# Two layers on eight cores: attention preparation and attention interleaved one to one, and three score banks re-dealt

## The reference

```python
# q, k, v: 16 heads, D = 64, S = 2048; BQ = BKV = 64, scale = D ** -0.5
def step(carry, kv):
    o, m, l = carry
    s = einsum('bhnqd,bhkd->bhnqk', qb, kj) * scale
    m_new = maximum(m, s.max(axis=-1))
    p = exp(s - m_new[..., None])
    alpha = exp(m - m_new)
    l_new = alpha * l + p.sum(axis=-1)
    o_new = (alpha[..., None] * o + einsum('bhnqk,bhkd->bhnqd', p, vj)) / l_new[..., None]
...
return out @ Wo
```

## Time and profile before

| | us |
|---|---|
| runs, median of 2 | 10,394.06 |
| lowest and highest run | 10,362.76 and 10,425.37 |
| profiled execution | 10,050.02 |
| its span on the slowest core (core 3) | 10,048.5 |
| spans of the eight cores | 10,022.2 to 10,048.5 |
| busy in the span: TensorE, VectorE, ScalarE | 7585.1, 4055.9, 2167.9 |

### The profile page before, as it was taken

How to read it: one execution, slowest core, us unless ns; L and a number is a source line. 1 busy time by engine, 2 the same in 40 slices (tenths; PEclk the granted TensorE clock), 3 DMA queues, 4 the chain that set the end, 5 groups by cost and what they waited for, 6 DMA issues and landing times. The chain is left out here.

```text
span 10048.5 us, 90480 instructions; the slowest of 8 cores (10022.2 to 10048.5 us)
## 1 busy us (share of the span) xinstructions
PE 7585.1 (75%) x30432; PEld 2823.7 (28%) x30432; DVE 4055.9 (40%) x7403; ACT 2167.9 (22%) x3617; POOL 209.7 (2%) x256
## 2 busy tenths in 40 slices
PE   1688888888426464563746547999999999999998
PEld 0233333333101111110111102444444444444443
DVE  6433333432564545546455452233332323232332
ACT  0100001001024243342423334111111212111111
POOL 0000000000000000000000000000000000000000
PEclk6699999999655555565565556999999999999999
DMA  1121221211000000000000000222222222222222
GB/s 37 16 31 26 31 33 26 34 30 27 10 0 4 3 4 4 2 4 1 4 5 2 3 0 13 38 34 37 36 36 36 35 37 35 37 36 34 38 34 63
DMA packets 224606, 229.20 MB, mean 23 GB/s; under 512 B 23200, under 2 KB 220960, under 8 KB 222112
## 3 DMA queue, kind: packets, MB, share of 16 engines
q0 software_dynamic: 221280, 206.49, 13.7%
q1 hardware_dynamic: 2880, 16.94, 0.5%
HBM read 421.49 MB, written 8.39 MB: 43 GB/s over the span
## 5 line engine op out<-in xcount | busy, mean ns | idle before, releaser
L1387 PE MATMUL f_yb<-hh,ring 128*128 128x512 bf16 x8192 | 1820.0, 379 | 63.8 <-DVEq L99 52.1
L1354 PE MATMUL f_h<-xn,ring 128*128 128x512 bf16 x8192 | 1794.9, 381 | 30.7 <-issue 21.9
L1362 ACT ACTIVATE hh<-f_h,b_sb 128x512 bf16<-128x512 f32 x1024 | 703.6, 687 | 3036.1 <-PE f_h L1354 3036.1
L1035 PE MATMUL atb<-k,q 64*128 64x512 bf16 x1024 | 563.5, 591 | 878.2 <-ACT es L1052 872.3
L1399 DVE TENSOR_TENSOR x_sb<-x_sb,f_yb 128x512 f32<-128x512 f32 x1024 | 703.7, 687 | 1224.4 <-PE f_yb L1387 838.3
L1354 PEld LDWEIGHTS f_h<-xn,ring 128*128 128x128 bf16 x8192 | 800.8, 98 | 1022.3 <-issue 80.5
L1387 PEld LDWEIGHTS f_yb<-hh,ring 128*128 128x128 bf16 x8192 | 777.3, 98 | 1041.4 <-issue 146.3
L1057 DVE TENSOR_REDUCE sg<-es 128x8 f32<-128x512 f32 x1024 | 702.3, 686 | 815.6 <-ACT es L1052 815.6
L1368 DVE TENSOR_TENSOR hh<-hh,gb_sb 128x512 bf16<-128x512 bf16 x1024 | 435.3, 425 | 1410.1 <-ACT hh L1362 1410.1
L1052 ACT ACTIVATE es<-atb 128x512 f32<-128x512 f32 x1024 | 611.5, 597 | 1765.5 <-DVE mu L1042 1765.5
L1042 DVE TENSOR_REDUCE mu<-atb 128x8 f32<-128x512 f32 x1024 | 698.8, 682 | 596.0 <-PE atb L1035 596.0
(11 more groups left out here) (187 smaller groups left out, 4558.2 us busy)
## 6 DMA issues: line engine op xcount, KB each, us to landing
ring<-l1w POOLq DMA_DIRECT2D x128, 1024.0 KB, 8.7
ring<-moe POOLq DMA_DIRECT2D x40, 1024.0 KB, 8.2
ring<-moe POOLq DMA_DIRECT2D x40, 512.0 KB, 6.8
x_sb<-xt SPq DMA_DIRECT2D x1, 8192.0 KB, 28.9
yt<-x_sb SPq DMA_DIRECT2D x1, 8192.0 KB, 23.1
ring<-wv POOLq DMA_DIRECT2D x4, 512.0 KB, 7.9
ring<-wq POOLq DMA_DIRECT2D x8, 256.0 KB, 4.9
ring<-wk POOLq DMA_DIRECT2D x8, 256.0 KB, 4.5
```

What stands on the lines that cost most here:

```text
L1035: p.t.emit(lambda t, rb0=rb0, qt=qt, kvc=kvc, SB_=SB_, tp=tp, pb=pb: t.matmul(SB_.t[:], q2[pb][rb0:rb0 + 64, qt * 128:(qt + 1) * 128], k2[ ...
L1354: p.t.emit(lambda t, k=k, ml=ml, c=c, i=i, h=h_w1: t.matmul(H1[i].t[:], ring.lhsT(h, k, ml * 128, 128), xnv(k, c), start=(k == 0), stop=(k ...
L1362: p.s.emit(lambda s, i=i, m=m, c=c, bcol=bcol: s.activation(hh1[:, m * T + c * CW: m * T + (c + 1) * CW], H1[i].t[:], AF.Gelu, bias=b1_sb[ ...
L1387: p.t.emit(lambda t, k=k, ml=ml, c=c, i=i, h=h_w2, fq=fq: t.matmul(YB[i].t[:], ring.lhsT(h, k, ml * 128, 128), hh1[:, k * T + c * CW: k * ...
```

## The change

Three edits in the attention phase. The ST items take the banks B[3], B[6] and B[7] in turn instead of B[6] and B[7]. The odd head's scores always go to B[2] instead of alternating between B[2] and B[3]. And run_interleaved takes one item of each generator in a round; before it took two of gen_prep and one of gen_st. Projections and transposes stay on B[6] and B[7], and no instruction is added or removed.

```diff
@@ gen_prep
-                            SB_ = B[6 + (sti % 2)]
+                            SB_ = (B[3], B[6], B[7])[sti % 3]
@@ gen_st
                         SE_ = B[i]
-                        SO_ = B[2 + i]
+                        SO_ = B[2]
@@ run_interleaved
-                alive_a, alive_b = a is not None, b is not None
-                while alive_a or alive_b:
-                    for _ in range(2):
-                        if alive_a:
-                            try:
-                                next(a)
-                            except StopIteration:
-                                alive_a = False
-                    if alive_b:
+                gens = [g for g in (a, b) if g is not None]
+                while gens:
+                    nxt = []
+                    for g in gens:
                         try:
-                            next(b)
+                            next(g)
+                            nxt.append(g)
                         except StopIteration:
-                            alive_b = False
+                            pass
+                    gens = nxt
```

## The result

| | before | after |
|---|---|---|
| runs, median (lowest to highest), us | 10,394.06 (10,041.03 to 11,128.27), 10 runs | 10,587.93 (10,362.11 to 11,447.02), 11 runs |
| profiled execution, us | 10,050.02 | 10,357.69 |
| its span on the slowest core | 10,048.5 | 10,356.1 |

The ratio of after to before is 1.0316, 95% interval [1.0297, 1.0334]: slower by 3.2%. In many executions of either kernel one die ran its dense stages at a lower clock; the ratio is taken over the executions without that, so it isn't the ratio of the two medians.

A forecast was written before the change was run, and what follows sets the result against it. Attention was taken as bound by a chain between engines, the period of one round. Units 1 to 7 at +270 and the last unit at +46.6 gave +317 on the 10,394 median: 10,710 us, range 10,570 to 10,830.

The forecast's parts named there:

- pair round: Round with a gen_st item of two kt steps beside gen_prep's ST work: 6.26 us before, 5.28 after at 1.2 GHz.
- ST item alone: One gen_prep step (matmul, max mu, exp es, sum sg) without attention work beside it: 2.07 us, unchanged.
- units 1 to 7 together: Four odd units at +41.9 us and three even units at +34.2: +270.
- attention alone, last unit: Last unit, no preparation beside it: 2.49 us per kt step, from 122.7 to 169 us, +46.6.
- full-clock rival: Pair rounds hold full clock: 4.16 us each, time 10,517 us, +1.2%; chance 10%.
- third bank: ST matmuls over three banks: worth nothing; its rival had shorter ST steps alone, 10,123 us, 2.6% faster; chance 4%.
- Projection rounds: Rounds with a gen_prep projection item beside two kt steps: 6.13 us before, 5.05 after, at full clock.
- third rival: Projection rounds lose the clock because S waits in them: +2.75 us each, 201 more, 10,912 us; chance 4%.
- end item: Last gen_st item of each query chunk, only O(15) and copies to o_pair: added 4.14 us before, 2.48 after.
- So odd takes 76.5 too: Odd units' tails and output go from 69.7 to 76.5 us, since output then lies beside ST steps.
- tails and output: Scans and transposes after each parity's ST items, plus output items: 69.7 us odd, 76.5 even before; 76.5 both after.
- Edit 2 costs up to 0.7 a round: Odd scores on the one bank B[2]: S waits for the previous pt_o, up to 0.7 us a round.

## Why the prediction was right, point by point

| term of the sum | forecast, us | measured, us |
|---|---|---|
| pair round, two to one to one to one | 6.26 to 5.28 | 6.25 to 5.29 (medians of 184 and 147) |
| ST item alone | 2.07, unchanged | 2.07 to 2.08, unchanged |
| units 1 to 7 together | +270 | +268.2 (2,998.6 to 3,266.9) |
| attention alone, last unit | +46.6 | +46.0 |
| total | +317 | +307.6 in the span, +314.2 in the stretch |

The clock in the pair rounds, the largest unknown, stayed at 1.2 GHz: 3 of 147 rounds are 4.18, near the 4.16 of the full-clock rival, directly behind projections. The rival's round was right in size, and it did not come about. The runs add why: what keeps the clock down in the changed kernel goes with the single bank. Without it, and with the same one-to-one order, 16 to 43 of 147 rounds are under 4.2, by core; with it, 0 to 3. That this is through TensorE's gap of 0.66 us a round is my reading; no run varied the gap alone, and the rounds of 4.57 stay at 0.50 with hardly a gap. So the cause of the clock's rise stays open.

The third bank was taken as nothing, and both runs, the one that takes it away and the one that adds it, agree within 3 us.

Three steps were off in size.

Projection rounds were forecast at 5.05 at full clock throughout. Steady ones are 5.07, but the third rival came true in a small part. Five starts in the timeline of the changed kernel:

```profile
3060.08 3.57 PE L998 MATMUL atb<-xn,ring 128*128 128x512 bf16 x8
...
3068.14 3.59 PE L1012 MATMUL atb<-xn,ring 128*128 128x512 bf16 x8
...
3075.12 1.90 PE L998 MATMUL atb<-xn,ring 128*128 128x512 bf16 x8
...
3080.19 1.90 PE L1012 MATMUL atb<-xn,ring 128*128 128x512 bf16 x8
...
3569.48 2.57 PE L1012 MATMUL atb<-xn,ring 128*128 128x512 bf16 x8 [2.40 <-DMA ring<-wk]
```

The first round lasts 8.06 us (3060.08 to 3068.14) at 1.2 GHz, where 7.8 was the bound, and the second 6.98; only then is it 5.07. The last row is in unit 2, behind the end item in round 9: TensorE waited 2.40 us for the load of wk, which I had not seen coming, and two rounds lost the clock again. (The kernel before waits there too, 2.95 us in unit 2, and keeps the clock.) From its first matmul to its first ST matmul unit 1 takes 46.3, 40.4 forecast; unit 2 takes 90.0, 78.2 forecast. The same stretches before were 26.1 and 55.9 against my 24.5 and 49.0. Over units 1 to 7 this part grew by 172 us, 151 forecast.

"So odd takes 76.5 too" is the second step that was off, and the one that hid the first. The sum gave tails and output 69.7 us in an odd unit before and 76.5 after, 76.5 in an even one. Measured from a unit's last product to the next unit's start, less the ST items at 2.07, they take 71.6 before and 71.4 after in odd units, 72.2 and 71.1 in even ones. Nothing was added in an odd unit: the 6.8 were the 6.9 by which the even unit's v and projection rounds had come out too small (55.9 against 49.0). That is 27 us too many, against 21 too few in the projection rounds, and that the two nearly cancel is luck. The +270 for units 1 to 7 is closer than its parts.

"Edit 2 costs up to 0.7 a round" is the third. At an unchanged clock it is right: 5.29 against 4.57 (medians) is 0.72, 106 us for 147 rounds. As the price of the single bank it is too small. It made 103 us in the pair rounds, 47 in the last unit and some 50 in projection rounds. The runs with and without it (the changed kernel with two ST banks, and one to one alone) differ by 241 to 278 us, core by core; on core 5 by 3,782.4 - 3,504.4 = 278. Of these, 150 are in the pair rounds (147 x (5.39 - 4.37), means), 56 in the last unit (from its first pt_e to its last, 163.8 against 108.2) and the other 72 in projection and end rounds. On the eight cores the pair rounds make 123 to 150. What this has over 106 is the clock, which rises in some rounds without the single bank, and which I had held fixed. This step was not in the sum, which used 5.28 as it comes out with all edits, so the total stands.

And the split is not a sum: one to one alone costs 33 to 77 us, the single bank alone 289, both 314, so on top of the single bank one to one costs only 25. Once the second S waits for pt_o, two es ahead of it cost a two-to-one round 1.1 us (7.37 against 6.25); one to one takes one es out, and the single bank costs its rounds 0.72.

One price among the rivals is off: cold projection rounds were counted as 28 in the odd units where the sum has 32, so that rival would cost 212 us and not 201.

## What to carry to other kernels

Work out a pipelined round from durations between starts, engine by engine in stream order, before believing a row of idle time: TensorE's repeated 1.49 us behind es looked like a lack of banks and was slack, and the 0.79 us of VectorE behind es was the bound. A bank that lets a producer run one step ahead can be worth more than its own wait says, because everything in the stream behind the wait moves with it: with the single bank alone TensorE's waits for pt_o grow by 247 us (254.6 to 501.7), the time by 289. Where one engine alternates between two sides of another engine's work (mu, es, sg), put the second half one item late; here that is worth 6 to 7%.

## What the hardware showed that I had not expected

VectorE starts a reduction over 128 x 512 F32 0.59 to 0.60 us after the start of the one before it while each lasts 0.68, so two took 1.19 us here and not the 1.38 that I added up from durations.

TensorE ran without gaps and still at 1.2 GHz. A window in the last unit of the kernel before (columns as in the earlier trace rows):

```profile
6066.00:6090.00 24.00, 24.00 (x72) 4.50 (x70) 0.00 (x0) 12.79 (x24) 0.00 (x0) 0.50 0.00 1
```

TensorE was busy for all 24 us, with half-array score matmuls in it, and the clock was 0.50; its rises to 1.00 came later in that unit. In the changed kernel's projection rounds, eight full-array matmuls and two kt steps each, the clock came up within two rounds (above, 8.06 and 6.98, then 5.07). The Trainium skill, TensorE: Matmul & The Clock Gate, "Part 1: The HAM clock gate", says that activity releases the throttle. The trace agrees in the projection rounds and not in this window, 24.00 us of busy TensorE at 0.50. In pair rounds whose gaps had closed (one to one alone), the clock rose in some rounds and not in others: in 16 to 43 of 147, by core. The runs do not show what decides it.
